# Order tables of a transformer block on one core: places, set-up order, delays and bank estimates replaced

## The reference

```python
xn = layernorm(x)                                  # x: 16 batches x 512 tokens x 256
x + attention(xn) + ffn(xn)
# attention: 8 heads of width 128; q, k, v = xn @ wq, wk, wv; rope on q and k;
#   s = q k^T / 128, causal mask, softmax, p @ v, then the projection by wo
# ffn: h = [xn, -xn]; relu(s0 * h @ K0) * 2; relu(s1 * h @ K1) * 2; s2 * h @ K2
#   K0: 512 x 1024, K1: 1024 x 1024, K2: 1024 x 256, each entry +1 or -1
```

## Time and profile before

| what | us |
|---|---|
| median of three timed runs | 1774.23 (1773.61 to 1775.03) |
| the profiled execution | 1775.91 |
| its span, first to last instruction | 1774.1 |
| PE busy | 1718.2 (97%) |
| DVE busy | 1534.4 (86%) |
| ACT busy | 1267.5 (71%) |
| POOL busy | 925.6 (52%) |
| mean granted TensorE clock | 0.998 of 2.4 GHz |

### The profile page before, as it was taken

How to read it: one execution, slowest core, us unless ns; L and a number is a source line. 1 busy time by engine, 2 the same in 40 slices (tenths; PEclk the granted TensorE clock), 3 DMA queues, 4 the chain that set the end, 5 groups by cost and what they waited for, 6 DMA issues and landing times.

```text
span 1774.1 us, 34030 instructions
## 1 busy us (share of the span) xinstructions
PE 1718.2 (97%) x12720; PEld 1194.3 (67%) x12720; DVE 1534.4 (86%) x3630; ACT 1267.5 (71%) x2717; POOL 925.6 (52%) x952
## 2 busy tenths in 40 slices
PE   6899989999999999999999999999999999999999
PEld 2356757767676676767767677676766767677667
DVE  8899888897988979888897988979889798888985
ACT  6677676776867677677776867768677776777763
POOL 6555545554545555465455555555456454655632
PEclk9999999999999999999999999999999999999999
DMA  5234543344343434334244333433434344433443
GB/s 172 48 54 73 93 69 78 66 79 81 57 96 60 84 66 71 79 67 91 53 85 83 64 81 67 78 76 63 91 60 88 67 66 85 67 86 58 79 74 69
DMA packets 454838, 134.08 MB, mean 76 GB/s; under 512 B 434704, under 2 KB 453648, under 8 KB 454672
## 3 DMA queue, kind: packets, MB, share of 16 engines
q1 hardware_dynamic: 454672, 131.90, 39.9%
HBM read 14.94 MB, written 8.39 MB: 13 GB/s over the span
## 4 chain that ended last, share of the span: by engine, by line
PE 67%; DVE 19%; ACT 5%; DMA 3%; POOL 3%; issue 2%; SPq 0%; DVEq 0%; POOLq 0%; ACTq 0%
PE bank L489 67%; DVE ph L703 3%; DVE p L666 3%; DVE bank L625 3%; DVE bank L617 2%; DVE qk L635 2%; DMA pt<-ph 2%; ACT p L680 2%; DVE rt L841 1%; POOL xT L319 1%; DVE v L543 1%; DMA xT<-rt 1%; POOL tb L621 1%; DVE hb L822 1%; DVE o L543 1%
## 5 line engine op out<-in xcount | busy, mean ns | idle before, releaser
L697 POOL TENSOR_SCALAR ph<-p,ri 128x384 f16<-128x384 f32 (+3 forms) x512 | 313.2, 612 | 453.9 <-DVE rk L687 416.7
L621 POOL TENSOR_TENSOR tb<-tb,sin 128x512 f32<-128x512 f32 x256 | 331.3, 1295 | 245.2 <-ACT tb L613 238.8
L489 PE MATMUL bank<-hb,wa 128*128 128x256 f16 x3360 | 379.9, 273 | 0.3 <-ACT bank L882 0.3
L489 PEld LDWEIGHTS bank<-hb,wa 128*128 128x128 fp8e5 x3360 | 327.9, 98 | 41.8 <-ACT bank L882 0.5
L680 ACT ACTIVATE p<-p,nm,sc 128x512 f32<-128x512 f32 (+3 forms) x512 | 328.6, 645 | 1.6
L703 DVE SCALAR_TENSOR_TENSOR ph<-p,rk,ph 128x512 f16<-128x512 f32 (+3 forms) x512 | 311.4, 616 | 0.7 <-POOL ph L697 0.7
L666 DVE CUSTOM_DVE_ANT_0 p<-bank,mask 128x512 f32<-128x512 f32 (+3 forms) x512 | 228.9, 484 | 49.9 <-PE bank L489 46.8
L489 PE MATMUL bank<-pt,v 128*128 128x256 f16 (+1 forms) x2304 | 233.1, 256 | 15.1 <-DMA pt<-ph 13.5
L489 PE MATMUL bank<-qk 128*128 128x512 f16 (+3 forms) x1536 | 229.9, 299 | 16.0 <-DVE qk L635 14.6
L489 PEld LDWEIGHTS bank<-pt,v 128*128 128x128 f16 x2304 | 202.6, 98 | 43.0 <-DMA pt<-ph 20.2
L489 PEld LDWEIGHTS bank<-qk 128*128 128x128 f16 x1536 | 132.8, 98 | 121.4 <-DVE qk L635 22.4
(11 more groups left out here) (107 smaller groups left out, 2259.2 us busy)
## 6 DMA issues: line engine op xcount, KB each, us to landing
out<-xnat SPq DMA_DIRECT2D x32, 256.0 KB, 2.4
xnat<-in_x SPq DMA_DIRECT2D x15, 512.0 KB, 3.8
pt<-ph SPq DMA_TRANSPOSE x256, 4.3
o<-in_k SPq DMA_DIRECT2D x1, 1024.0 KB, 7.2
v<-in_wq SPq DMA_DIRECT2D x1, 1024.0 KB, 9.2
v<-in_wk SPq DMA_DIRECT2D x1, 1024.0 KB, 10.9
ph<-in_wv SPq DMA_DIRECT2D x1, 1024.0 KB, 13.5
o<-in_wo SPq DMA_DIRECT2D x1, 1024.0 KB, 10.2
```

What stands on the lines that cost most here:

```text
L489: self.todo.append(lambda e, stop=False: e.matmul(self.ps[:, cols[0]:cols[1]], lhsT, rhs, start=first, stop=stop, skip_group_check=skip))
L621: done["crossed", n] = pool.put(lambda e: e.tensor_tensor(tb, tb, SIN[:], ALU.mult))
L697: done["P_hi", g, i] = pool.put(lambda e: e.tensor_scalar(part(r, i, HI), v, RI[:, g % 4, i:i + 1], 4096.0, ALU.mult, ALU.mult))
```

## The change

It replaces numbers in the tables, and the order in `FIRST`; no instruction is added, removed or resized. The whole diff:

```diff
--- before.py
+++ after.py
@@ -51,57 +51,57 @@
 
 
 PLACES = {
-    "l1_2": ((5, 2),),
-    "l1_3": ((7, 1),),
-    "l1_4": ((2, 2),),
-    "l1_5": ((0, 5),),
-    "l1_6": ((1, 2),),
-    "l1_7": ((1, 4),),
-    "v_0": ((6, 5),),
-    "v_1": ((-1, 5),),
-    "v_2": ((0, 0),),
-    "v_3": ((1, 2),),
-    "v_4": ((4, 1),),
-    "v_5": ((2, 5),),
-    "v_6": ((2, 4),),
-    "v_7": ((3, 3),),
-    "l0_1": ((2, 2), (3, 0), (3, 5), (5, 2)),
+    "l1_2": ((7, 5),),
+    "l1_3": ((9, 0),),
+    "l1_4": ((1, 3),),
+    "l1_5": ((-2, 2),),
+    "l1_6": ((1, 3),),
+    "l1_7": ((1, 5),),
+    "v_0": ((8, 2),),
+    "v_1": ((-3, 0),),
+    "v_2": ((-3, 4),),
+    "v_3": ((5, 5),),
+    "v_4": ((4, 0),),
+    "v_5": ((2, 4),),
+    "v_6": ((2, 5),),
+    "v_7": ((3, 2),),
+    "l0_1": ((2, 2), (3, 0), (3, 5), (5, 3)),
     "l0": ((-2, 4), (0, 2), (0, 5), (1, 1)),
     "v0_1": ((-4, 4), (-3, 5), (-2, 3), (-2, 2)),
-    "v0": ((-3, 5), (-3, 1), (-1, 0), (0, 4)),
+    "v0": ((-3, 5), (-3, 0), (-1, 0), (0, 4)),
     "v1": ((3, 5), (4, 1), (4, 0), (1, 4)),
-    "seg_1": ((-1, 2), (-1, 3), (0, 5), (2, 5), (3, 3), (4, 0), (4, 1), (4, 2)),
-    "seg": ((2, 2), (2, 3), (3, 2), (3, 3), (3, 3), (4, 0), (4, 2), (5, 4)),
-    "seg_15": ((2, 0), (3, 4), (4, 1), (4, 2), (5, 2), (5, 4), (5, 5), (6, 5)),
+    "seg_1": ((-2, 3), (-1, 3), (0, 5), (2, 5), (3, 3), (4, 0), (4, 1), (4, 4)),
+    "seg": ((2, 2), (2, 5), (3, 2), (3, 3), (3, 3), (4, 0), (4, 2), (5, 2)),
+    "seg_15": ((2, 0), (4, 0), (4, 1), (4, 2), (5, 2), (5, 4), (5, 5), (6, 4)),
     "l2_0": ((2, 3), (4, 4)),
-    "l2": ((6, 3), (8, 3)),
-    "l2_15": ((8, 2), (7, 0)),
-    "proj": ((9, 0), (9, 3)),
+    "l2": ((6, 2), (8, 3)),
+    "l2_15": ((8, 2), (7, 2)),
+    "proj": ((9, 1), (9, 3)),
 }
 
 
-SETUP = dict(v_max=96.7, o_max=51.6, a11=46.8, a12=45.5, a22=71.6, s1a=1.2, s1b=18.9, s2a=4.8, s2b=11.7, s3a=4.9,
-             s3b=1.6, s4a=73.7, s4b=89.9, k2=59.9, x1=129.6, wq1=87.8, wk1=113.9, wq2=87.4, wk2=120.1, wq3=107.7,
-             wk3=131.5, wv0=120, wv1=92.1, pads=108.1, ascale=156.1, wo0=146.2, wo1=152.5)
-FIRST = ("am0", "l1", "p0", "l1", "qk", "qk", "qk", "am2", "l1", "qk", "p2", "l1", "S", "qk", "S", "l1", "qk", "l1",
-         "v", "v", "v", "v")
-
-
-EARLY = dict(qhi=(23.8, 21.1, 24.7), qlo=(22.9, 20.4, 17.8), bias=(6.3, 7.5, 7.4), exp=(7.3, 2.6, 5.3),
-             inv=(14.5, 0, 10.9), high=(2.7, 14.3, 15.5), low=(20.6, 36.1, 24.1), turned=(42.8, 23.7, 43.6),
-             rotated=(13.8, 15.3, 11.9))
+SETUP = dict(v_max=86.2, o_max=52.7, a11=49.9, a12=46, a22=70.1, s1a=0.7, s1b=30.9, s2a=0, s2b=13.9, s3a=1.9,
+             s3b=2.8, s4a=72.9, s4b=99.7, k2=61, x1=138.3, wq1=87, wk1=115.7, wq2=88.2, wk2=124.6, wq3=118.7,
+             wk3=125.1, wv0=119.3, wv1=90.5, pads=105.1, ascale=141.5, wo0=145.9, wo1=161.5)
+FIRST = ("l1", "am0", "l1", "p0", "qk", "qk", "am2", "qk", "qk", "l1", "p2", "l1", "S", "qk", "S", "qk", "l1", "v",
+         "v", "l1", "v", "v")
+
+
+EARLY = dict(qhi=(23.8, 23.1, 24.7), qlo=(25.2, 18.4, 17.8), bias=(8.4, 7.0, 7.0), exp=(5.7, 2.6, 5.6),
+             inv=(15.2, 0.1, 10.9), high=(2.7, 14.5, 10.8), low=(23.8, 36.1, 25.8), turned=(38.0, 23.0, 37.4),
+             rotated=(14.5, 15.3, 11.2))
 LAST = ((-1, range(0, 5)), (0, range(5, 7)), (1, range(7, 8)))
 
 
-DELAY = dict(hi=0, lo=11.3, swap=0, straight=9.6, crossed=0, rotated=15.5, qhi=21.8, qhi_w=0, qlo=19.8, bias=8.1,
-             exp=11.6, exp_i=1.4, differ=4.7, keep_hi=0, keep_lo=17.4, t_hi=10.6, t_lo=18.1, add=7, inv=23.5,
-             high=22.6, high_i=6.1, low=43.7, low_i=8.3, turned=66.6, x_hi=48.8, x_lo=60.5, x_turned=70.7)
-
-
-HELD = dict(am=0, p2=23.2, T=30.9, qk=30.5, S=8.2, PV=23.0, v=13.7, l0=25.3, l1=18.3, seg=21.5, l2=18.6, proj=8.7)
-
-
-LATE = dict(rotated=14.1, qhi=19.3, qlo=22.0, bias=4.9, exp=11.3, inv=19.6, high=36.1, low=33.0, turned=46.4)
+DELAY = dict(hi=0, lo=12, swap=0, straight=9.6, crossed=0.1, rotated=14.9, qhi=21.8, qhi_w=0, qlo=20.4, bias=8.1,
+             exp=11.6, exp_i=1.4, differ=4.7, keep_hi=0, keep_lo=20.4, t_hi=12.1, t_lo=18.8, add=7, inv=23.3,
+             high=23.4, high_i=5.9, low=43.7, low_i=8.3, turned=87.7, x_hi=47.7, x_lo=61.3, x_turned=71.3)
+
+
+HELD = dict(am=1.0, p2=12.8, T=30.1, qk=29.9, S=12.1, PV=22.0, v=17.7, l0=23.5, l1=23.4, seg=26.2, l2=15.8, proj=5.7)
+
+
+LATE = dict(rotated=13.9, qhi=21.9, qlo=21.9, bias=8.1, exp=9.6, inv=5.9, high=42.0, low=38.8, turned=42.2)
 
 
 class Queue:
```

## The result

| | before | after |
|---|---|---|
| median (lowest to highest), us | 1774.41 (1773.61 to 1775.19), 7 runs | 1780.16 (1777.78 to 1781.57), 7 runs |
| ratio | 1 | 1.0031, 95% interval 1.0020 to 1.0043 |
| profiled execution, its span, us | 1775.91, 1774.1 | 1780.16, 1778.4 |

The time lies outside the forecast range, on the other side of no change. The span grew by 4.3 us. One of 120 further runs of the kernel before took 2528 us at a mean granted clock of 0.668 and is left out of all that follows. Here are the page's busy times of the kernel after and its stretches; the columns are those of the earlier trace rows.

What follows compares the result with a forecast made beforehand. PE was taken as full, busy 1718.2 of 1774.1 us, so only its waits could be won: 0 + 0 - 3.5 - 1.3 + 0 = -4.8 us, from 1774.2 to 1769.4 us, range 1760 to 1779.

Steps and rivals of the forecast that it cites:

- Slots, 0; DELAY, 0: Steady batches: new places and delays cost 0, as no distance behind a PE wait changes; ends -17.7 and +18.
- (a): Start: no l1 covers the 3.5 us between p0's matmul and the first q projection any more, +3.5 us.
- HELD, 0: Choice of other banks: taken as 0, since PE hardly waits for a bank's reader; ends -1 and +14.7 us.
- slower: banks: Rival: a fill of each batch meets a bank DVE still reads, +14.7 us, giving 1784 us; chance 0.15.
- (b): Start: am2's 3.72 us wait becomes about 1.2, as o's largest-entry instruction on DVE comes earlier, -2.5 us.
- (e): Start: head 1's second k projection comes 3.5 us earlier, removing the 2.95 us wait of its scores, -2.9 us.
- (f): Start, scores of head 2: POOL's sine product goes ahead of batch 1's layernorm, -3.1 us.
- (d): Start: p2's wait of 1.72 us for three small DVE instructions stays unchanged.
- (c): Start: the new 3.5 us gap can lower the clock as the old am2 wait did (1.7 us), so 0.
- Sum of the start, -3.5: Up to 180 us: PE's side gives -5.4, cut to -3.5 because DVE is nearly full; ends +4 and -9.
- given back: Rival: DVE's total up to 163 us counts, new holes replace old ones, -1, 1773 us; chance 0.27.
- Batch 1, -1.3: Batch 1: of 6.2 us lost, a shorter second wait saves 1.3 us; ends -6.2 and +2.

Runs made afterwards that it cites:

- f3: The kernel before with only the new HELD table: 1774.86 us, ratio .9999.
- e1: The kernel before with only the new start tables (FIRST, SETUP, EARLY): 1776.33 us, ratio 1.0007 to before.
- g3: The kernel after with the whole old PLACES table back: 1776.47 us, ratio 1.0004 to before.
- g4: e1 with the three small DVE instructions that p2 needs queued right behind am2: 1775.43 us, ratio .9995 to before.
- e4: The kernel after with 20 extra overwritten matmuls on PE ahead of its wait for p2's scale: 1778.33 us, ratio 1.0020 to before.
- e3: The kernel before with only the new DELAY table: 1774.62 us, ratio 1.0000.

## Why the prediction was wrong, by its steps

- **Slots, 0; DELAY, 0: the step that failed first.** It took 0 "since no distance behind a wait of PE changes". That argument only sees consumers that wait. The places moved no such distance, and still the order of fills shifted DVE against POOL by 0.1 us, which turned a pair that excludes each other. Cost: two collisions, twice 1.5 us on PE, 1.2 and 1.5 in the steps, of which some 0.6 came back, with shorter waits for `pt`. The range for slots and delays (-17.7 to +18) held it; the value didn't.
- **What could have been read before.** The trace of before had the effect in the open: L703 at 0.74 with POOL's L621 stretched to 1.75 beside it, 0.12 us apart, in nine of fifteen batches. Step (a) also took 3.5 us from a row that held such a stretch: DVE's first split of wq took 2.29 us beside POOL's ffn sums in before, and 0.98 in after, where POOL's sum ended 0.43 us into it. So the gap was 2.23, not 3.5, and the wait for wk, 0.95, did not stay.
- **HELD, 0: right**, by f3. The rival "slower: banks" had the right sign; its 1784 is 4 us above what came, with a mechanism that f3 shows absent in the steady state. One bank wait did grow, at 76 us in the start.
- **(b) am2 1.2: it is 0. (e) -2.9: that wait went** (2.95 to 0), but the scores of head 1 start no earlier, since p2 took it all. **(f) -3.1: failed.** POOL's product is ahead of the layernorm as said and its wait goes (2.59 to 0.42), but the bank wait behind it grows by 1.9, so the two are 0.3 us shorter together.
- **(d) p2 "unchanged": failed**, 1.72 to 5.78 us. I looked at what p2 waits for and not at DVE's queue ahead of it: as many projections as before precede p2, but with an `l1` between them and p2 more of their rope is due first (2.0 us), and DVE's split of wq now takes 1.7 us longer beside POOL's sine products.
- **(c) the clock, 0: the step that failed in the start and in batch 1.** There is half clock in three stretches of the start instead of one, and for 6.8 us instead of 3.4 in batch 1. The first two show no cost at 87 us, since DVE is behind anyway up to there. The third, at 79.4 us, stands where PE sets the pace again, and its 1.4 us stay. (c) looked only at the gap behind am2 and the new one of (a).
- **Sum of the start, -3.5: failed.** It is +1.1 us at 101 us in the trace and 1.1 us in the mean of e1 and of g3. The cap by DVE was right in kind and too generous: with PE's waits taken away in g4 and e4, the reciprocal of head 2 comes at 87.2 and 86.4 us, against 87.0 in after. That is the rival "given back" for this stretch.
- **Batch 1, -1.3: failed**, its wait is 3.51 for 3.46 and the half clock behind it longer: +0.9 us.
- **The marker "steady idle 1.2 to 1.5 us a batch"** held (19.8 over 13 is 1.5) and told nothing: 2 us more in two batches is far under what it could see. "On the same two waits" did fail, with hb.

In the two traces this adds up to 1.1 in the start, 0.9 in batch 1 and 2.1 in the steady batches, 4.1 us of the 4.3. Open: the second edit beside the last part's place; what makes the bank wait of 2.95 us and the half clock behind it, where all five traces with the new start tables have an L703 of 128 columns that takes 2.20 or 2.31 us beside POOL's L581, and which no run changes alone; and how often other executions of these kernels collide, since one was traced of each.

## What to carry to other kernels

When the order of work changes, look for pairs of a DVE instruction with two SBUF inputs and a GpSimd instruction that start within 0.2 us of each other; the loser stands for the rest of the other's instruction, and the trace shows that as a longer instruction, never as a wait. Compare the lengths of the same instruction between two traces before comparing waits, then ask whether PE waits for what stands behind the longer one. A wait of PE that goes in a stretch where DVE is 90% busy is not won: follow the stretch to its end, and see where the gain is left. At that end, compare the lengths of the same matmuls too: a lowered clock costs nothing while PE would wait anyway, and its full price from the moment that PE sets the pace.

## What the runs showed of the hardware

- L703 128x512 takes 0.74 us alone, 1.80 when POOL's 1.27 us product starts with it, 1.58 when that started 0.23 us earlier, 1.25 beside a product of half the columns: each time it ends 0.55 us behind POOL's instruction. With POOL 0.12 us behind it is 0.74, and POOL's takes 1.75.
- Half clock is granted for 3.4 or 6.8 us around PE's longer waits, and the same order of work on PE had it once behind am2 for 3.4 us (before) and once for 6.8 (e3), with a time of 1774.6 all the same. Behind the bank wait at 79 us it cost what the 12 matmuls took longer, 1.4 us in after and 2.6 in g4. The Trainium skill (TensorE: Matmul & The Clock Gate, Why this matters for your kernels) warns of idle gaps; here waits of 2.59 to 2.95 us at 54 and 75 us had it in some kernels and not in others, and the one of 3.5 us at 240 had 3.4 or 6.8 us of it, so a single profile does not give a gap's price.
